# Two transformer layers with adaptive layer norm: the residual stream kept with tokens on partitions, gates as rows, and a spread moved on SyncE

## The reference

```
mod = (silu(c) @ wmod).reshape(16, 6, 1, 128)
sa, ca, ga, sb, cb, gb = mod[:, 0], ..., mod[:, 5]
ga = (2 * (ga >= 0) - 1) * max(abs(ga), 0.25)        # gb the same
h = layernorm(x) * (1 + ca) + sa
x = x + ga * attention(h)                            # ends in y @ Wproj + bproj
h = layernorm(x) * (1 + cb) + sb
x = x + gb * experts(h)
```

## Time and profile before

| What | us |
|---|---|
| Median of 3 runs | 1263.21 |
| Lowest and highest | 1258.15, 1270.37 |
| Span of the profiled execution | 1264.6 |
| Opening | 0 to 49.7 |
| First attention | 49.7 to 452.0 |
| First norm phase | 452.0 to 482.4 |
| Routing and experts of layer 0 | 482.4 to 709.8 |
| Middle phase | 709.8 to 784 |
| Sparse attention | 784 to 945 |
| Norm phase, routing, experts of layer 1 | 945 to 1240 |
| Last phase | 1240 to 1264.6 |

### The profile page before, as it was taken

How to read it: one execution, slowest core, us unless ns; L and a number is a source line. 1 busy time by engine, 2 the same in 40 slices (tenths; PEclk the granted TensorE clock), 3 DMA queues, 4 the chain that set the end, 5 groups by cost and what they waited for, 6 DMA issues and landing times. The chain is left out here.

```text
span 1264.6 us, 40174 instructions
## 1 busy us (share of the span) xinstructions
PE 1049.0 (83%) x16287; PEld 831.3 (66%) x16287; DVE 811.1 (64%) x1610; ACT 812.6 (64%) x1799; POOL 677.7 (54%) x695
## 2 busy tenths in 40 slices
PE   7789999999999864699776497899976679999983
PEld 5567777777777752698666353555545569988872
DVE  6578777877778757410000375899976937666775
ACT  6356556555556543687666473677765579998984
POOL 7656687676687510377777301232320068888861
PEclk9789999999999976799999698799997789999997
DMA  4622222222221025111112500000005511111117
GB/s 130 164 45 49 51 47 45 52 48 45 45 50 16 4 43 175 37 53 52 51 53 52 151 1 1 5 5 7 5 4 143 175 38 43 46 48 45 46 32 206
DMA packets 112505, 72.97 MB, mean 58 GB/s; under 512 B 44065, under 2 KB 102785, under 8 KB 112193
## 3 DMA queue, kind: packets, MB, share of 16 engines
q1 hardware_dynamic: 103232, 51.77, 18.0%
q0 software_dynamic: 9088, 18.63, 5.0%
HBM read 51.84 MB, written 17.71 MB: 55 GB/s over the span
## 5 line engine op out<-in xcount | busy, mean ns | idle before, releaser
L2057 ACT ACTIVATE act_x_m<-ps_h_x_m,fc_bias_x_m 128x256 f32<-128x256 f32 (+1 forms) x480 | 184.5, 464 | 68.8 <-PE ps_h_x_m L1996 62.7
L970 ACT ACTIVATE probT<-ps_t 128x512 f32<-128x512 f32 (+1 forms) x208 | 118.9, 594 | 139.7 <-PE ps_t L824 138.4
L1996 PE MATMUL ps_h_x_m<-x_T_x_m,fc_x_m 128*128 128x256 f32 (+1 forms) x960 | 205.0, 364 | 4.3 <-ACT x_T_x_m L2065 2.3
L2168 POOL DMA_INDIRECT x_rows_x_m<-h_dram,token_m x142 | 140.3, 988 | 106.8 <-POOLq L1692 67.3
L1996 PEld LDWEIGHTS ps_h_x_m<-x_T_x_m,fc_x_m 128*128 128x128 f32 x960 | 166.4, 195 | 23.8 <-issue 6.1
L2015 PE MATMUL ps_o_x_m<-proj_x_m,act_x_m 128*128 128x128 f32 x1136 | 143.7, 278 | 34.8 <-DVE y_x_m L2103 27.2
L2178 POOL DMA_INDIRECT y_dram<-y_x_m,dest_m x142 | 142.6, 1005 | 48.2 <-issue 40.9
L2015 PEld LDWEIGHTS ps_o_x_m<-proj_x_m,act_x_m 128*128 128x128 f32 x1136 | 133.1, 192 | 44.5 <-ACT act_x_m L2057 26.8
L746 POOL TENSOR_TENSOR rel_y<-rel_raw,own_rows 128x1024 f32<-128x1024 f32 x64 | 130.6, 2041 | 45.0 <-ACT rel_raw L978 45.0
L922 DVE TENSOR_REDUCE neg_max<-ps_s 128x8 f32<-128x512 f32 (+1 forms) x64 | 95.4, 1491 | 89.8 <-PE ps_s L809 89.8
L2103 DVE TENSOR_TENSOR y_x_m<-ps_o_x_m,out_rows_m 128x256 f32<-128x256 f32 (+1 forms) x40 | 15.8, 394 | 164.4 <-DMA y_dram<-y_x_m,dest_m 120.7
(11 more groups left out here) (315 smaller groups left out, 2139.0 us busy)
## 6 DMA issues: line engine op xcount, KB each, us to landing
q_spread<-q_dram SPq DMA_DIRECT2D x256, 64.0 KB
got_m<-y_dram SPq DMA_DIRECT2D x32, 256.0 KB, 4.7
h_dram<-h_rows_m SPq DMA_DIRECT2D x16, 256.0 KB, 2.3
x_rows_x_m<-h_dram,token_m POOLq DMA_INDIRECT x142, 2.6
y_dram<-y_x_m,dest_m POOLq DMA_INDIRECT x142, 2.3
x_rows<-L_attn_x SPq DMA_DIRECT2D x8, 256.0 KB, 4.1
q_dram<-qT SPq DMA_DIRECT2D x8, 256.0 KB, 9.3
fc_all_m<-L_ffn_c_fc SPq DMA_DIRECT2D x8, 256.0 KB, 5.3
```

The lines of the kernel that those rows point to most:

```text
L970: act.activation(probT[to:to + n, store(m, ch), :, (2 * j + s) % 4, :], ps_t[row:row + n, t % 2, :].rearrange("p (g c) -> p g c", g=GROUPS ...
L1996: m = pe.matmul(ps_h[:, l, g, f % 2, 0:w], fc[:, slot, l, f * P:(f + 1) * P], x_T[:, slot % 2, 0:w], start=True, stop=True)
L2057: m = act.activation(out[:, slot % 2, f, 0:w], ps_h[:, l, g, f % 2, 0:w], ACT.Tanh if l else ACT.Gelu, scale=0.5 if l else 1.0, bias=fc_bi ...
L2168: pool.indirect_dma_start(out=x_rows[:, slot, h, :], out_offset=None, in_=k.h_dram, in_offset=bass.IndirectOffsetOnAxis(ap=r.token[:, c:c ...
```

## The change

The residual stream is `k.x`, 128 partitions x 32 tiles x 128 channels with tokens on partitions, and is never turned. `open_phase` loads into it directly. `k.mod` keeps the four vectors of shift and scale. The gates are made as rows, 16 batches on partitions: PE multiplies the condition with the gate columns of `wmod`, DVE does five steps on them and a sixth that multiplies the projection's bias by the gate. SP writes both layers' rows (gate, gate times bias, second gate) to `gate_dram` between its stores of q. Later phases read them back as broadcast rows, the same row on all partitions.

- Opening: PE's `rows_in`, ACT's `copy_x` and DVE's `gate_bias` are gone, and `spread(sp, a, 1)` is now the first thing on SP in the attention.
- First attention: for each batch SP fetches 128 KB of broadcast rows; POOL multiplies `wproj` by the gate and adds the gated bias to x (`gate_weights`); PE projects with y as stationary operand, 128 tokens at a time, so that the output has tokens on partitions; DVE adds it to x from PSUM and makes the statistics of the finished tiles into `k.moments`. ACT's gate and POOL's add are gone.
- First norm phase (`counted`): no transposes in, no statistics, one root and one reciprocal for all 32 tiles, and DVE normalises all chunks from SBUF. PE turns back chunk n and makes rows of chunk n-1.
- Norm phase of layer 1: no transposes in; statistics by DVE from SBUF, odd chunks by ACT as before, chunk n-1 is normalised while n is measured.
- Middle phase: `combine`, `to_rows` and DVE's add are gone. POOL multiplies `both` by the gate and adds it to x, two steps of 128x512 a chunk, the first chunk ahead of its constants. SP fetches 1 MB of broadcast gates ahead of the chunks 2 to 7. The norm reads x from SBUF.
- Sparse attention: 2 MB of broadcast rows first on SP; POOL's `gate_weights` for each batch; two PE products in the projection; ACT's gate is a plain copy; POOL adds it to x.
- Last phase: PE does nothing. SP fetches 1 MB of gates first, ACT and DVE weigh, POOL multiplies by the gate, DVE adds to x, SP stores from x.

```diff
-            spread(sp, a, 1)
             for n in range(1, NCH):
                 store_q(n)
+                if n in (3, NCH - 2):
+                    l = int(n > 3)
+                    sp.wait_ge(gates_done, l + 1)
+                    sp.dma_start(k.gate_dram[:, l, :, :], gate_rows[:, l, :, :]).then_inc(gates_out, 16)
+            sp.wait_ge(gates_out, 32)
...
             dve.wait_ge(table_in, 16 * TABLES)
-            dve.tensor_scalar(a.gate_bias[:, :], k.mod[:, 0, 2, :], a.bproj[:, 0:1], None, ALU.mult)
...
+            def gate_rows(b):
+                wait(sp, wproj_ready, b - 1)
+                wait(sp, x_biased, b - 1)
+                sp.dma_start(gates[:, b % 2, :, :], bass.AP(k.gate_dram.tensor, 6 * C * b, [[0, P], [1, 2 * C]])).then_inc(gates_in[b % 2], 16)
+
+            spread(sp, a, 1)
             for b in range(2, B):
                 if b % 2 == 0:
                     sp.wait_ge(a.q_out[b // 2], 16)
                 sp.wait_ge(a.rel_ready, b - 1)
+                gate_rows(b - 2)
                 spread(sp, a, b, score)
...
-            def add(b):
-                pool.wait_ge(gated, b + 1)
-                xs = k.xT[:, b * T:(b + 1) * T]
-                pool.tensor_tensor(xs, xs, upd[:, b % 2, :], ALU.add).then_inc(added, 1)
+            def gate_weights(b):
+                pool.wait_ge(gates_in[b % 2], 16 * (b // 2 + 1))
+                wait(pool, projd, b - 1)
+                pool.tensor_tensor(wproj[:, b % 2, :], a.wproj[:, :], gates[:, b % 2, 0, :], ALU.mult).then_inc(wproj_ready, 1)
+                xs = k.x[:, 2 * b:2 * b + 2, :]
+                pool.tensor_tensor(xs, xs, view(gates[:, b % 2, 1, :], 0, [[0, 2], [1, C]]), ALU.add).then_inc(x_biased, 1)
...
                 if half == 0:
-                    wait(pe, gated, b)
+                    wait(pe, added, b)
...
                 pe.wait_ge(y_ready, b + 1)
-                pe.matmul(ps_y[:, 0, :], a.wproj[:, :], y_T[:, b % 2, :], start=True, stop=True).then_inc(projd, 1)
+                pe.wait_ge(wproj_ready, b + 1)
+                for u in range(2):
+                    x = pe.matmul(ps_y[:, 0, u * P:(u + 1) * P], y_T[:, b % 2, u * P:(u + 1) * P], wproj[:, b % 2, :],
+                                  start=True, stop=True, skip_group_check=True)
+                x.then_inc(projd, 1)
...
+            def add(b):
+                dve.wait_ge(projd, b + 1)
+                dve.wait_ge(x_biased, b + 1)
+                xs = k.x[:, 2 * b:2 * b + 2, :]
+                dve.tensor_tensor(xs, ps_y[:, 0, :].rearrange("p (u c) -> p u c", u=2), xs, ALU.add).then_inc(added, 1)
...
+                if j == 0 and b >= 2:
+                    add(b - 2)
+                if j == 1 and b >= 2:
+                    statistics(b - 2)
+            statistics(B - 1)
...
+            sp.dma_start(gates[:, :, :], bass.AP(k.gate_dram.tensor, 2 * C, [[0, P], [6 * C, B], [1, C]])).then_inc(gates_in, 16)
             for n in range(LEAD, NCH):
                 choice_rows(sp, k, r, n)
...
+            def add(n):
+                pool.wait_ge(both_ready, 4 * (n + 1))
+                if n == 0:
+                    pool.wait_ge(gates_in, 16)
+                y = both[:, n % 2, :, :]
+                pool.tensor_tensor(view(both[:, n % 2, 0, :], 0, [[2 * C, 2], [C, 2], [1, C]]),
+                                   view(both[:, n % 2, 0, :], 0, [[2 * C, 2], [C, 2], [1, C]]),
+                                   view(gates[:, 2 * n, :], 0, [[C, 2], [0, 2], [1, C]]), ALU.mult).then_inc(gated, 1)
+                pool.wait_ge(gated, n + 1)
+                xs = k.x[:, 4 * n:4 * n + 4, :]
+                pool.tensor_tensor(xs, xs, y, ALU.add).then_inc(added, 1)
...
             def add(n):
-                dve.wait_ge(combined, n + 1)
-                for s in range(2):
-                    b = 2 * n + s
-                    xs = k.xT[:, b * T:(b + 1) * T]
-                    m = dve.scalar_tensor_tensor(out=xs, in0=ps_c[:, n % 2, s * T:(s + 1) * T], scalar=k.mod[:, 1, 5, b:b + 1],
-                                                 in1=xs, op0=ALU.mult, op1=ALU.add)
-                m.then_inc(added, 1)
+                dve.wait_ge(gated, n + 1)
+                xs = k.x[:, 4 * n:4 * n + 4, :]
+                dve.tensor_tensor(xs, xs, both[:, n % 3, :, :], ALU.add).then_inc(added, 1)
```

466 lines of the change are left out of this document (228 added, 238 removed).

## The result

The changed kernel is slower: a median of 1270.31 us over 20 runs (1265.52 to 1280.13) against 1266.28 (1258.15 to 1270.62) for the kernel before, over 20 runs too. The ratio is 1.0045, with a 95% interval of 1.0025 to 1.0065. I had forecast 5 us less and it became 4 more. The median lies inside the range that I gave, 1250 to 1271, but at the end that a rival had set, and on the other side of the kernel before. The profiled execution has a span of 1268.1 us against 1264.6.

A forecast was written before the change was run, and what follows sets the result against it. No single engine bounds the kernel; barriers close each phase, so each counts by its last wait. Terms −3.2, 0, −8, −1, +4.2, 0, +2.6 sum to −5.4: 1259.2 us span, 1257.8 by median, 1258.5 said; range 1250 to 1271.

The forecast's parts named there:

- The step that failed: Middle and last phases: POOL's and DVE's steps run side by side; +4.2 us and +2.6 us forecast there.
- the other case as a rival: POOL's products hold up DVE's two-input steps: +9.5 us middle phase, +5.8 last, 1267.7 us on the span; chance 0.22.
- stay under: Last phase: DVE's weighing (about 1.26 us) and sum (0.6 to 0.7) stay under ACT's 2.0 us steps.
- its 5.3 us for the holds: Middle phase, in POOL's hold rival: DVE's shift and weighing wait some 1.05 us in five chunks, +5.3 us.
- the low clock as a rival of its own: First norm phase: clock never rises, steps stay 3.1 us, −1 instead of −8, 1266.2 us on the span; chance 0.12.
- Fetch: Middle phase: 1 MB of gates ahead of the rows delays chunk 2's rows and the first normalise by 3.8 us.
- First norm phase: Ready statistics and no transposes in shorten this phase: −8 us, range −10 to −1.
- the tail: First norm phase, after the last turn back: 4.6 us before, gives up little, 3 to 4.6 us.
- ACT loses its gate step: First attention: ACT's gate step goes, DVE's added work fits into gaps; 0 us, range −1 to +4.
- Opening: Spread transfers leave SP, so its stores follow q at once: −3.2 us, range −2 to −4.
- my 46.5: Opening: the first attention starts at 46.5 us, where it began at 49.73 before.
- Sparse attention: POOL's gate steps (1.15 us a batch) go into 6.34 us of idle time: 0 us, range −1 to +3.

The follow-up runs named there:

- the run with the shift ahead: Changed kernel with DVE's reciprocal and shift put ahead of its weighing in the middle phase: 1258.42 us in one run, middle phase 81.2 us.
- the run with one row: Changed kernel fetching only batch 0's gate row (64 KB instead of 1 MB) in the middle and last phases, used for all batches: 1267.42 us.
- the last run: Changed kernel, shift ahead, gates fetched early, last product on DVE, gate store not awaited, DVE's gate steps behind the opening's last statistics: median 1254.21 us, ratio 0.9895.

## Why the prediction was wrong

**The step that failed** is the one of the middle and last phases that took POOL's two steps and DVE's as running side by side. I had the other case as a rival, at 0.22, and let one row decide against it: a sum of two SBUF inputs at 36.80 that took 0.20 us with POOL busy. That row stood beside a one-input POOL step. The rows that pointed the other way, DVE steps at 32.37 and 45.93 that ended with a POOL product, were of the very kind of POOL step that the change adds. The rule of the Trainium skill (SBUF — State Buffer, "Who interferes with whom") said the same, and I weighed it against a row that didn't test it. After the change both are seen: beside POOL's one-input steps the two-input DVE step of 16x256 at 26.78 in the opening takes 0.43 us and isn't held, beside POOL's products shifts and weighings are. In the last phase the failed line is that DVE's weighing and sum "stay under" 2.0 us a chunk: they take 2.66.

**The rival itself was sized too low.** It had +9.5 in the middle phase and +5.8 in the last; measured were +14.8 and +8.9. In the middle phase its 5.3 us for the holds was near (five of 1.0 to 1.1 and one of 0.5, 5.8 in all). What was missing is what follows: PE waits longer in each step, its clock falls to 0.5 for part of the time, and the stretched step is stretched again, another 3.5 us by the run with the shift ahead. I had the low clock as a rival of its own, in the first norm phase, where it cost nothing against the forecast (mean 0.75, 0.78 before). The steady loop kept 1.7 us more than before even without the holds, where I had put 0.4. In the last phase the fetch cost 4.0 to 5.3 us by two runs, not 3.7, and the holds a microsecond each in five weighings and the first sum.

**Fetch.** +3.8 to the first normalise of the middle phase; 3 to 4 by the run with one row. Right.

**First norm phase.** −8 predicted, −9.6 measured. (The parts as I gave them end at 475, which is −7.5.) To the first turn back I had 3 us (455 − 452), measured 3.5; for the seven steps 16.9, measured 13.1; for the tail 3, measured 4.2. Right in size, and the statistics ahead with what goes with them are its cause, as the run without them shows. What I gave to the removed transposes is not borne out: without the statistics ahead nothing is gained.

**First attention.** 0 predicted, −7 to −9 measured. The failed term is "ACT loses its gate step", which I put at nothing: an ACT step of 0.4 us a batch and the wait for it, put back, bring 5 to 9 us back. The wait itself is a small part, as PE's values begin 2.25 us after the projection in either kernel; how the rest comes about stays open. DVE's added work, 1.0 us a batch (299.17 us before, 314.66 now), did fit into its gaps.

**Opening.** −3.2 predicted, +2.1 in the profiled pair. That SP held the old end is right: in both executions of the kernel before the next phase begins 0.4 us after SP's last store is issued (49.32 and 55.34). But SP got a new wait, for the landing of two stores of 24 KB behind 256 KB stores, which I had said would fall into time in which SP isn't last: it is worth 1.6 to 1.9 us. Another 2.8 us of the 5.3 by which the start missed my 46.5 is POOL's masking, which I had ending at 46.77 and which ended at 49.54, as the first spread came later. Its start varies between executions of either kernel (42.27 and 45.76 before, 42.7 to 45.9 after), so the change need not be the cause. DVE's six gate steps take about 0.4 us, not 0.20, as they are of 16x256 elements (256 to a partition, 32 before), and stand ahead of statistics for which POOL then waits 1.43 us; whether that counts stays open.

**Others.** Norm phase of layer 1: −1, as said. Sparse attention: −2.1 against 0, but it is 158.3 to 160.4 in different executions with the changed kernel's code there, so chance can have made it. The end of the last phase, from DVE's last weighing through POOL's product and DVE's sum, took 2.45 us (1262.90 to 1265.35) where I had 1.85, as that product is held too.

## What to carry to other kernels

Work that moves to an idle POOL is free for DVE only where POOL doesn't read SBUF with a product while DVE has steps of two SBUF inputs; where it must, let DVE's short steps that others wait for stand ahead of the step that releases POOL, as two lines in another order gave back 8 us here. Moving a DVE step to another time can bring it beside such a product, as the 4.56 us in the last run show. A row that is to clear a resource has to show the same pair of instructions, not a similar one. And a fetch that is constant over a phase belongs into the phase before, where the transfers have room: 1 MB ahead of the rows cost 3 to 5 us in each of two places, and nothing that can be seen when issued earlier.

## What the runs showed of the hardware

A DVE step of 0.16 us took 1.24 beside a POOL product of 128x512 (1.26 us), and four weighings 2.13 instead of 1.13; beside POOL MEMSETs they took 1.16. The longest hold was of a step of 0.41 us: 4.56 beside POOL's product of 128x2048 (4.48 us). POOL was held by DVE as well: 1.65 us instead of 1.24 for the product that began beside DVE's sum of 128x512. Beside POOL steps with one tensor input (128x128 TENSOR_SCALAR, 0.8 us each) DVE steps of two SBUF inputs weren't held (0.43 and 0.41 us for 16x256, 0.41 with POOL idle), though those POOL steps read SBUF too; small delays there were, as a gate step of 0.28 us with POOL idle took 0.37 and 0.46. I hadn't expected that a hold of 1.1 us in a step of 7 would cost 2.4: PE was idle for 1.9 to 2.0 us before the turns to columns at 724.58 and 743.56, and after each the granted clock fell from 1.00 to 0.50 for some microseconds. With DVE's hold gone it stayed at 1.00 through windows in which PE waited 0.3 to 0.75 us at a time. A 1 MB broadcast of 512 B rows was usable 7.6 and 8.2 us after its issue, with rows of the experts queued beside it. A store of 24 KB behind stores of 256 KB landed 7.6 us after its issue in one execution, 5.0 and 11.7 in two others.
